# Adapter layer with per-language weights: second products two pairs behind instead of three, another order of setup

## What is computed

```python
w1 = W1[language_ids]                                  # 512 x 128 for each sequence
w2 = W2[language_ids]                                  # 128 x 512
h = relu(einsum('bsh,bha->bsa', x, w1) + b1[ids])
y = x + einsum('bsa,bah->bsh', h, w2) + b2[ids]
mean, var = over the last axis of y
out = x + (y - mean) * rsqrt(var + 1e-5) * gamma[ids] + beta[ids]
```

## Time and profile before

| what | value |
|---|---|
| median of 3 runs | 325.13 us |
| profiled execution, its own time | 325.01 us |
| span in its profile | 323.3 us |
| TensorE busy | 298.4 us (92%) |
| VectorE busy | 308.6 us (95%) |
| ScalarE busy | 240.5 us (74%) |
| GpSimd busy | 186.0 us (58%) |
| mean granted TensorE clock | 0.984 |

### The profile page before, as it was taken

How to read it: one execution, slowest core, us unless ns; L and a number is a source line. 1 busy time by engine, 2 the same in 40 slices (tenths; PEclk the granted TensorE clock), 3 DMA queues, 4 the chain that set the end, 5 groups by cost and what they waited for, 6 DMA issues and landing times. The chain is left out here.

```text
span 323.3 us, 8131 instructions
## 1 busy us (share of the span) xinstructions
PE 298.4 (92%) x2199; PEld 270.8 (84%) x2200; DVE 308.6 (95%) x679; ACT 240.5 (74%) x605; POOL 186.0 (58%) x217
## 2 busy tenths in 40 slices
PE   2549999999999999999999999999999999999961
PEld 2139899999999999999999999999999999999940
DVE  5878999999999999999999999999999999999996
ACT  4937678777787777877778777787777877778752
POOL 2960764566655566555665556655566555665553
PEclk9968999999999999999999999999999999999997
DMA  4999988666777667766677666776667666433324
GB/s 160 305 354 428 379 297 262 243 228 237 253 240 233 233 221 259 242 225 231 217 252 240 233 233 218 260 245 217 235 219 262 231 228 235 156 132 133 130 109 152
DMA packets 41711, 75.69 MB, mean 234 GB/s; under 512 B 2253, under 2 KB 7404, under 8 KB 41542
## 3 DMA queue, kind: packets, MB, share of 16 engines
q1 hardware_dynamic: 41571, 75.04, 68.2%
q10 hardware_dynamic: 99, 0.14, 0.2%
HBM read 41.62 MB, written 33.55 MB: 233 GB/s over the span
## 5 line engine op out<-in xcount | busy, mean ns | idle before, releaser
L295 POOL TENSOR_TENSOR x_io<-x_io,beta_all 128x512 f32<-128x512 f32 x128 | 161.5, 1284 | 0.0
L403 PE MATMUL ps_h<-w_all,x_T 128*128 x1024 | 143.2, 283 | 0.0
L403 PEld LDWEIGHTS ps_h<-w_all,x_T 128*128 128x128 f32 x1024 | 125.7, 193 | 1.5
L342 ACT ACTIVATE cut<-ps_y,row_sum 128x512 bf16<-128x512 f32 x128 | 87.9, 687 | 22.2 <-PE ps_y L430 22.2
L573 DVE SCALAR_TENSOR_TENSOR x_io<-ps_y,rstd,x_io 128x512 f32<-128x512 f32 x128 | 90.2, 747 | 2.5 <-DVE rstd L565 0.3
L320 ACT COPY x_T<-ps_T 128x512 f32<-128x512 f32 x128 | 74.0, 578 | 23.5 <-PE ps_T L395 23.4
L560 DVE SCALAR_TENSOR_TENSOR ps_y<-ps_y,mean,gamma_all 128x512 f32<-128x512 f32 x128 | 90.7, 753 | 0.7 <-ACT cut L342 0.4
L395 PE MATMUL ps_T<-identity,x_io 128*128 128x128 f32 x512 | 78.6, 277 | 10.7 <-DMA x_io<-in_x 10.7
L292 POOL TENSOR_TENSOR mean<-row_sum,over_h 128x2 f32<-128x2 f32 x64 | 13.0, 203 | 124.6 <-DVE ps_y L541 113.7
L541 DVE SCALAR_TENSOR_TENSOR ps_y<-x_io,b_all 128x512 f32<-128x512 f32 x124 | 83.0, 710 | 0.0
L395 PEld LDWEIGHTS ps_T<-identity,x_io 128*128 128x128 f32 x512 | 63.2, 143 | 20.1 <-issue 11.6
(11 more groups left out here) (60 smaller groups left out, 171.4 us busy)
## 6 DMA issues: line engine op xcount, KB each, us to landing
x_io<-in_x SPq DMA_DIRECT2D x64, 512.0 KB, 4.4
out<-x_io SPq DMA_DIRECT2D x63, 512.0 KB, 3.0
x_io<-in_L_cond_W SPq DMA_DIRECT2D x5, 512.0 KB, 7.2
w_all<-in_L_cond_W SPq DMA_DIRECT2D x5, 512.0 KB, 8.7
b_all<-in_L_cond_b SPq DMA_DIRECT2D x1, 2560.0 KB, 15.1
out<-x_io SPq DMA_DIRECT2D x2, 256.0 KB, 2.0
x_io<-in_L_cond_gamma SPq DMA_DIRECT2D x1, 60.0 KB
x_io<-in_L_cond_beta ACTq DMA_DIRECT2D x1, 60.0 KB
```

Of the source, the lines that this page charges most:

```text
L295: nc.gpsimd.tensor_tensor(x_slot(t), x_slot(t), of_lang(beta_all, langs[b]), ALU.add)\
L342: nc.scalar.activation(squares[:, t % 2, :], ps_y[t % Y_BANKS][:, :], ACT.Square, scale=-float(H), bias=stat(row_sum, t), accum_out=stat(s ...
L403: last = nc.tensor.matmul(part, x_T[:, t % 4, c, :], w1_all[:, bass.ds(lang, 1), c, :].rearrange("p o a -> p (o a)"), start=False, stop=(c ...
```

## The change

The second products of pair p now run two pairs behind its first ones (FIRST = 2), and h has five buffers for pairs instead of six. In VectorE's step `low_h(n + 1)` stands between `scale_pair(n)` and `invert_pair(n)`, where `low_h(n + 2)` stood behind `finish_pair(n)`. In ScalarE's step `high_h` comes ahead of both copies. Both b1 matmuls of a pair stand ahead of the pair's first product; only the first of them starts the bank. Three parts of W2 are loaded ahead of W1. W1 is loaded with rows 2k and 2k+1 of a block of 256 in one partition, so that a run is 1 KB where it was 512 B, and `turn_x` takes every second column of x to match. In setup, beta's rows are issued ahead of b1's, and the order of the means, high and low parts of W2 is another.

```diff
-H_PAIRS = 6
-FIRST = 3
+H_PAIRS = 5
+FIRST = 2
 EARLY = 2
-W2_AHEAD = 2
+W2_AHEAD = 3
...
-                sp.dma_start(w1_all[:, langs, :, :], w1[langs].rearrange("l (c p) a -> p l c a", p=128)).then_inc(s_w1, 16)
+                sp.dma_start(w1_all[:, langs, :, :].rearrange("p l (k j) a -> p l k (j a)", j=2),
+                             w1[langs].rearrange("l (k p j) a -> p l k (j a)", p=128, j=2)).then_inc(s_w1, 16)
...
+            act.dma_start(x_io[0:3 * L, 2 * ROWS_PAIR + 1, :],
+                          beta.unsqueeze(0).broadcast_to([3, L, H])).then_inc(s_beta_rows, 16)
             act.dma_start(b1_rows[:, :],
                           b1.unsqueeze(0).broadcast_to([3, L, A])).then_inc(s_b1_rows, 16)
-            act.dma_start(x_io[0:3 * L, 2 * ROWS_PAIR + 1, :],
-                          beta.unsqueeze(0).broadcast_to([3, L, H])).then_inc(s_beta_rows, 16)
...
             def step(p):
 
+                high_h(p - 1)
                 if p < PAIRS - 1:
                     copy_x(2 * p + 2)
-                if p > 0:
-                    high_h(p - 1)
-                if p < PAIRS - 1:
                     copy_x(2 * p + 3)
                 copy_h(p)
...
-                    last = nc.tensor.transpose(ps_T[t % 2][:, c, :], x_io[:, t % SLOTS, c * 128:(c + 1) * 128],
+                    last = nc.tensor.transpose(ps_T[t % 2][:, c, :], x_io[:, t % SLOTS, c // 2 * 256 + c % 2:(c // 2 + 1) * 256:2],
...
+            def h_sums(t):
+                return pair_of(ps_h)[:, (t % 2) * A:(t % 2 + 1) * A]
+
+            def put_b1(p):
+
+                for b in range(2):
+                    nc.tensor.matmul(h_sums(2 * p + b), of_lang(pick, langs[p][b]), b1_parts[:, :],
+                                     start=(b == 0), stop=False, skip_group_check=True)
+
             def first_product(t, lang):
-                part = pair_of(ps_h)[:, (t % 2) * A:(t % 2 + 1) * A]
-                nc.tensor.matmul(part, of_lang(pick, lang), b1_parts[:, :], start=True, stop=False)
...
-                    if b == 0 and p > 0:
-                        turn_h(p - 1)
+                    if b == 0:
+                        if p > 0:
+                            turn_h(p - 1)
+                        put_b1(p)
                     first_product(2 * p + b, langs[p][b])
...
+                if p is not None:
+                    low_h(p)
                 invert_pair(n)
                 finish_pair(n)
-                if p is not None:
-                    low_h(p)
```

More of the change, by code:

```diff
@@ L365, in _ @@
                 copy_spread(n)
-            for n in range(W2_AHEAD):
+            for n in range(2):
                 high_w2(n)
@@ L369, in _ @@
                 copy_spread(n)
+            high_w2(2)
             copy_x(2)
             copy_x(3)
-            high_w2(2)
+            high_w2(3)
             copy_h(0)
@@ L375, in _ @@
             high_h(0)
-            high_w2(3)
+            high_w2(4)
             copy_x(5)
             copy_h(1)
-            high_w2(4)
-            step(2)
             for p in range(FIRST, PAIRS):
@@ L394, in turn_x @@
                 for c in range(C):
-                    last = nc.tensor.transpose(ps_T[t % 2][:, c, :], x_io[:, t % SLOTS, c * 128:(c + 1) * 128],
+                    last = nc.tensor.transpose(ps_T[t % 2][:, c, :], x_io[:, t % SLOTS, c // 2 * 256 + c % 2:(c // 2 + 1) * 256:2],
                                                identity[:, :])
                 last.then_inc(x_turned, 1)
+            def h_sums(t):
[4 more added lines that the diff above has]
+                                     start=(b == 0), stop=False, skip_group_check=True)
             def first_product(t, lang):
-                part = pair_of(ps_h)[:, (t % 2) * A:(t % 2 + 1) * A]
-                nc.tensor.matmul(part, of_lang(pick, lang), b1_parts[:, :], start=True, stop=False)
                 for c in range(C):
-                    last = nc.tensor.matmul(part, x_T[:, t % 4, c, :],
+                    last = nc.tensor.matmul(h_sums(t), x_T[:, t % 4, c, :],
                                             w1_all[:, bass.ds(lang, 1), c, :].rearrange("p o a -> p (o a)"),
-                                            start=False, stop=(c == C - 1))
+                                            start=False, stop=False, skip_group_check=True)
                 if t % 2 == 1:
@@ L576, in _ @@
             dve.wait_ge(over_h_ready, 2)
-            for n in range(W2_AHEAD):
-                mean_of_w2(n)
+            mean_of_w2(0)
+            mean_of_w2(1)
             for n in by_dve:
@@ L581, in _ @@
                 nc.vector.tensor_copy(spread_to(n), spread_bank(n)).then_inc(spread_dve, 1)
-            for n in range(W2_AHEAD):
-                low_w2(n)
             mean_of_w2(2)
+            low_w2(0)
+            low_w2(1)
+            low_w2(2)
             mean_of_w2(3)
-            low_w2(2)
             mean_of_w2(4)
+            low_w2(3)
             low_h(0)
-            low_w2(3)
             seed_early(0)
@@ L596, in _ @@
             seed_early(1)
-            low_h(1)
             dve.wait_ge(s_b2, 16)
```

## The result

The changed kernel takes 328.04 us (median of 4 runs, 327.78 to 328.40) against 325.21 for the kernel before in the same session (4 runs, 324.71 to 325.93): a ratio of 1.0068, with a 95% interval of 1.0038 to 1.0099. It is slower, and it lies above the range that was given, 319.4 to 325.2. The profiled execution took 327.87 us, 2.86 more than that of before.

The account below looks back on a forecast made before the run. TensorE's 4.49 us period was taken to bound the loop, with VectorE close behind at 4.42. Start -3.1, one period more +4.50 and end -3.67 made -2.2 us: 322.8 us, range 319.4 to 325.2.

Parts of the forecast that it names:

- the low part of h between scale and reciprocal: VectorE's loop order: same work, hitches just covered, so costed at nothing, up to 0.9 us for all hitches.
- 0.8 us to spare: Loop: h's low part can end at 154.97, and TensorE wants it at 155.76.
- Strided columns at no cost: TensorE's transposes of x: every second column taken as free; upper bound twice 0.11 us each.
- slower: the strided transposes: Rival, chance 0.08: 8 strided transposes per pair cost time; from 7.6 ns each, over 0.5% slower.
- b1 side by side: TensorE's loop: pairing b1 matmuls taken as 0, bounds -0.055 and +0.055 us a pair.
- b1 in a pair saves a step: Rival on TensorE's period, chance 0.14: the paired b1 matmuls save 3.4 us, giving 319.4.
- The start: Setup until pair 0's second product: 30.9 against 33.96, -3.1 us, VectorE's and TensorE's paths both meeting at 31.
- VectorE's path: Start: means, low parts of W2 and h, and seeds summed on VectorE to 30.8, second product at 30.9.
- The end: Tail: last reciprocal 11.3 us after pair 61's second product (T), against 14.97 after pair 60's before, -3.67 us.
- one period more: Lag of two: 61 periods between second products instead of 60, +4.50 us, against -3.67 at the end.
- the marks that were set: Trace signs: second product at 30.9, period 4.49, four transposes 0.43, no h_low waits in loop, W1 over 300 GB/s.
- no waits of TensorE for h_low in the loop: Sign in TensorE's loop: it should never wait there for h's low part.

Follow-up runs that it names:

- e4: Changed kernel with VectorE's register load moved behind h's low part: 326.64 us, 1.0009 of the kernel before.
- e6: Changed kernel with the register load behind h's low part, W1 in 512 B runs and plain transposes: 323.06 us, 0.9885 of the kernel before.
- e1: Changed kernel with b1's rows issued ahead of beta's again: 327.75 us, 1.0044 of the kernel before.
- e5: Changed kernel with W1 in 512 B runs and plain transposes again: 328.04 us, 1.0039 of the kernel before.
- e8: Changed kernel with W1 in 512 B runs, plain transposes and each b1 matmul ahead of its own product: 328.42 us, 1.0064 of the kernel before.
- e12: Kernel before with b1 side by side, lag of two, register load behind h's low part, setup of before: 323.97 us, 0.9942 of the kernel before.
- e10: Changed kernel, register load behind h's low part, b1's rows first, two W2 parts ahead, 512 B runs, plain transposes: 326.51 us, 1.0011 of before.
- e11: Kernel before with W1 in 2 KB runs and transposes of every fourth column: 328.18 us, 1.0079 of the kernel before.

## Why the prediction was wrong

The step that failed first is the sentence "I cost it at nothing" on **the low part of h between scale and reciprocal**. It took VectorE's pace over from before, 4.42, because the work is the same. The order is not: the register load used to stand ahead of the reciprocal and mostly ended 0.1 to 0.3 ahead of the scaling (median 0.58 us long), so it cost nothing; now it stands ahead of h's low part, mostly lasts 1.19, ends only with the scaling, and holds h's low part back by 0.10 to 0.12. 4.42 + 0.12 = 4.54, and the 0.07 of room that the earlier trace rows showed was gone. The "0.8 us to spare" for h's low part was an offset at one moment. An engine that is slower by 0.03 a pair uses up any such offset; here that was so well before the middle of the run. e4 and e6 show this.

**Strided columns at no cost** failed next, and this was the rival "slower: the strided transposes" with a chance of 0.08. Its own number was right: from 7.6 ns each it is over 0.5% slower, and the transposes cost 9. The bound from both sides was wide enough; the choice of zero within it leaned on nothing in this trace.

**b1 side by side** was taken as zero and measures -0.05 a pair, its lower bound (-0.055). As the rival "b1 in a pair saves a step" it had 0.14. In the changed kernel it only pays most of the stride: 4.493 - 0.05 + 0.07 = 4.51, TensorE's own period. Since VectorE sets 4.54, it isn't seen in the time.

**The start**, -3.1, became -1.06. Data was not the limit: W1 moved at 357 GB/s for 352. What failed is VectorE's path taken as one sum. By it h's first low part starts at 27.6 (23.4 + 2.8 + 1.41); it started at 29.76. Its terms: the third mean 1.7 late (18.30 for 16.6); the six low parts of W2 0.7 shorter, because the 3.97 for four in the kernel before held more than twice the 1.41 of two; 0.64 for ScalarE's high part, 0.69 for h_high. The last two I had left out, and they decide: h_high comes at the end of TensorE's transposes of h and ScalarE's cast, whenever VectorE is there. The two seeds and two low parts behind it end only at 32.76. The paths don't meet at the end, they cross in the middle. TensorE's loop started at 22.39, where I had 21.71, held by copies of beta on ScalarE, and that moved the crossing along: by an estimate from this trace 0.7 of the 2.0 us is the late loop and 1.3 the crossing itself. In the six kernels with the new order of setup and three parts of W2 ahead (the changed one, e1, e4, e5, e6, e8) the first second product comes 9.6 to 10.8 us after the loop's first transposes, while those transposes start anywhere from 21.9 to 24.3. By itself TensorE would have been there at 31.74, its two turns taking 9.35 for 9.2. (21.71 + 9.2 is 30.9, not the 30.8 of my sum.) The lower granted clock of this stretch (0.57 from 20 to 26 us, 0.50 before) was in the forecast.

**The end**, T + 11.3, measured 11.84: 0.41 of it lies ahead of the last second product. VectorE went from scaling to scaling in 4.50 there (312.08 to 316.58) where I took 4.42, and its first scaling came at T + 2.09, not 1.96; from h's low part's end to TensorE's start it is 0.24 (318.31 to 318.55), for which I had 0.03. That one period more stands against a shorter tail was right.

Against the marks that were set: second product at 32.9 and not 30.9; period 4.51 to 4.56 and not 4.49; four transposes 0.47; 357 GB/s. The marks told the causes apart as they should. Only "no waits of TensorE for h_low in the loop" was a bad one: the list of waits has just two, both at the end (0.3 and 2.6 us), though VectorE sets the pace. Where two engines arrive within a tenth of a microsecond the list is empty, and only each engine's own period shows who leads.

Three versions with right products are faster than the kernel before: b1 side by side alone (322.76 us, 0.9914); e12 (323.97, 0.9942); and the lag of two with b1 side by side, the new order of setup, plain transposes and the register load moved (323.06 us, 0.9885). The intervals of their ratios overlap.

Open: what makes a register load last 1.2 us here and 0.5 to 0.6 in e4 and before; what the collision of the two cuttings costs (G); and how much the new order of setup is worth by itself (0.9 us by two medians whose intervals overlap).

## What to carry to other kernels

When two engines run within 2% of each other, write each one's period down on its own, with every instruction on it, register loads too, before costing an edit: an offset at one moment is not room, and undoing one of two near-equal costs shows nothing. Where an edit needs a form that the trace doesn't show (here a strided operand), and a change has several parts, time the parts apart: of three costed at zero here, two were the losses and one, b1 side by side, a gain of 0.9%. A sum along one engine's queue holds only if nothing in that queue waits for the others; look for the first such instruction and start the sum there. And before reading the start of one trace, compare its granted clock with that of the other.

## What the runs showed of the hardware

- A float32 weight load of 128 columns for a transpose took 143 ns from neighbouring columns, 203 from every second and 205 from every fourth; 9 ns of it reached the path.
- VectorE's register load of the language numbers ran beside the scaling and took 0.52 to 1.25 us in the changed kernel (median 1.19), 0.58 before and 0.53 in e4. What stood behind it did not start before it had ended: h's low part 1.42 to 1.45 after the scaling's start where the load ended only with the scaling, 1.32 where it ended 0.3 earlier; the reciprocal of before mostly 1.33, and 0.7 later behind a load of 1.44. Behind the low part, in e4, it cost 0.04.
- Two bf16 matmuls side by side took 0.11 us, as much as two apart, but the float32 product that had one ahead of it and now follows transposes took 0.81 instead of 0.86.
- VectorE's cast of 30 x 512 took 0.41 us alone and 0.80 to 1.30 while GpSimd cut another table of that size.
- TensorE's granted clock fell to 0.50 (1.2 GHz) in the start of the traces, not always at the same place: at 20.9 us in the changed kernel, at 14 in e1. In e10 it fell again, to 0.50 from 31 to 35 us, after TensorE had stood 3.6 us for h.
- From 10 to 18 us, while W1 moved, it was 285 to 298 GB/s in the seven kernels with runs of 512 B, 351 to 357 in the six with 1 KB and 383 in e11 with 2 KB. The Trainium skill, "DMA: Bandwidth & Descriptors", section Specifications, has 512 B as enough for line rate; the runs don't agree.
